# A four-layer graph network on one core: the edge loop spread over more steps, second maps set apart, aggregates with a second buffer

## The reference, cut to what matters

```python
h = act(edge_scalars @ fcW1 * c)
w = h @ fcW2 * c                      # 192 weights for each edge
xs, xv = f_s[edge_src], f_v[edge_src] # first map of the source node
edge_feat = products of w, xs, xv and edge_attr   # 4 x 96 numbers
agg = jax.ops.segment_sum(edge_feat, edge_dst, num_segments=n)
conv = second map of agg
x = _layernorm(x + combine(self map of x, conv), axis=-1)
```

## Time and profile before

| | |
|---|---|
| median of 3 runs | 4588.22 us (4581.89 to 4590.08) |
| the profiled execution | 4606.82 us, span 4605.1 us |
| busy shares of the span | PE 77%, PEld 69%, DVE 59%, ACT 47%, POOL 52% |
| instructions | 99292 |
| TensorE's mean granted clock | 0.902 |
| edge stages, about | 70 to 800, 1210 to 1965, 2315 to 3080, 3410 to 4200 us |

### The profile page before, as it was taken

How to read it: one execution, slowest core, us unless ns; L and a number is a source line. 1 busy time by engine, 2 the same in 40 slices (tenths; PEclk the granted TensorE clock), 3 DMA queues, 4 the chain that set the end, 5 groups by cost and what they waited for, 6 DMA issues and landing times.

```text
span 4605.1 us, 99292 instructions
## 1 busy us (share of the span) xinstructions
PE 3557.9 (77%) x23534; PEld 3169.8 (69%) x23534; DVE 2735.3 (59%) x11380; ACT 2167.5 (47%) x5622; POOL 2414.6 (52%) x2869
## 2 busy tenths in 40 slices
PE   3677778566577777889967777789987887787887
PEld 2677767566576777777756666677766777777776
DVE  3455555788644444578844444458865555555887
ACT  0223223566422222367733333347764444445888
POOL 1555555788555555466645555530015555555776
PEclk9788888888888888899978888989989999999999
DMA  9411122777411111278821111238861111113776
GB/s 355 157 42 43 45 47 60 233 252 255 129 32 39 42 42 42 53 249 291 289 57 37 40 43 42 47 117 298 298 193 31 34 40 41 40 43 128 259 261 231
DMA packets 424040, 572.49 MB, mean 124 GB/s; under 512 B 219010, under 2 KB 242340, under 8 KB 419618
## 3 DMA queue, kind: packets, MB, share of 16 engines
q1 hardware_dynamic: 295170, 322.46, 23.2%
q0 software_dynamic: 81680, 114.98, 9.8%
q10 hardware_dynamic: 47088, 133.90, 7.4%
HBM read 356.10 MB, written 233.79 MB: 128 GB/s over the span
## 4 chain that ended last, share of the span: by engine, by line
PE 37%; another core or an unknown queue 18%; ACT 13%; issue 13%; DVE 12%; DMA 4%; ACTq 2%; DVEq 1%; POOL 0%; SPq 0%; POOLq 0%
PE bank L799 7%; ACT arena L1071 5%; PE bank L830 4%; PE bank L828 4%; PE bank L838 3%; PE bank L806 3%; DVE stats L1425 3%; PE bank L852 3%; PE bank L829 2%; PE bank L787 2%; ACT nT L1045 2%; DVE arena L1418 1%; PE bank L907 1%; DVE mv L1436 1%
## 5 line engine op out<-in xcount | busy, mean ns | idle before, releaser
L584 POOL DMA_INDIRECT aggregates<-arena,meta x784 | 798.9, 1019 | 1083.4 <-ACT arena L993 344.1
L1071 ACT ACTIVATE arena<-arena,shift,rstd 128x160 f32<-128x160 f32 x1600 | 697.2, 508 | 64.9 <-DVE shift L1356 63.0
L571 POOL DMA_INDIRECT xg<-x_after,meta x588 | 584.3, 994 | 264.7 <-issue 258.4
L799 PE MATMUL bank<-same_all,msg 128*128 (+1 forms) x4704 | 644.6, 291 | 1.2 <-issue 1.2
L799 PEld LDWEIGHTS bank<-same_all,msg 128*128 128x128 f32 x4704 | 615.6, 209 | 1.7 <-issue 0.4
L1272 DVE SCALAR_TENSOR_TENSOR carry<-carry,meta,bank 128x3 f32<-128x3 f32 x784 | 170.7, 218 | 669.1 <-ACT arena L978 402.6
L978 ACT ACTIVATE arena<-bank 128x381 f32<-128x381 f32 x784 | 368.5, 492 | 357.9 <-remote 199.2
L828 PE MATMUL bank<-w,arena 128*128 128x98 f32 (+1 forms) x1568 | 373.7, 324 | 179.7 <-issue 89.2
L806 PE MATMUL bank<-nT,weights 128*128 128x128 f32 x1176 | 230.4, 308 | 345.2 <-ACT nT L972 269.5
L828 PEld LDWEIGHTS bank<-w,arena 128*128 128x128 f32 x1568 | 297.0, 218 | 283.7 <-issue 231.7
L1425 DVE BATCH_NORM_STATS2 stats<-arena 128x6 f32<-128x160 f32 x1600 | 453.5, 314 | 41.9 <-DVE arena L1418 10.0
(11 more groups left out here) (169 smaller groups left out, 7842.9 us busy)
## 6 DMA issues: line engine op xcount, KB each, us to landing
arena<-aggregates SPq DMA_DIRECT2D x400, 324.0 KB
x_after<-arena ACTq DMA_DIRECT2D x300, 320.0 KB
arena<-x_after SPq DMA_DIRECT2D x300, 320.0 KB
aggregates<-arena ACTq DMA_DIRECT2D x25, 1296.0 KB
arena<-nodes SPq DMA_DIRECT2D x100, 320.0 KB
out<-arena SPq DMA_DIRECT2D x100, 320.0 KB
same_all<-sorted_dst SPq DMA_DIRECT2D x7, 1792.0 KB, 13.3
aggregates<-arena,meta POOLq DMA_INDIRECT x784
```

The source lines that it names most:

```text
L571: gp.indirect_dma_start(xg[:, k % XGR, 4 + t * F:4 + (t + 1) * F], None, xtab[l], at).then_inc(gathered[k], 16)
L584: gp.indirect_dma_start(agg, at, tot[:, kk % TRING, t, 0:AW], None, bounds_check=NP - 1, oob_is_err=False).then_inc(spread[kk], 16)
L799: last = nc.tensor.matmul(bank[5 + t][:, c * P:(c + 1) * P], sent[:, c * P:(c + 1) * P], same_all[:, bass.ds(here[t], P)], start=True, sto ...
L1071: last = nc.scalar.activation(row, row, ACT.Identity, bias=shift[:, kk, t:t + 1], scale=rstd[:, kk, t:t + 1])
```

## The change

TensorE's step now works on four pairs: T and H of pair q, W and F of pair q-1, S of pair q-3, M0 and M1 of pair q-4, in the order T, S, M0, W, F, M1, H. ScalarE's step follows it: T's copy of pair q, the sums of pair q-3, the totals of pair q-4 (the first ahead of layer 3's gating of pair q-1, the second behind it), and the activation of pair q last. `aggT` has two buffers, and the copy into it waits for M of pair q-5 in place of q-3. VectorE completes the messages of pair q first and mends pair q-2 (before: pair q-1) behind that. The loops of TensorE and ScalarE are two steps longer, VectorE's one. GpSimd's and SyncE's code is the same. No product, copy or transfer is added or removed.

```diff
-                    has_new, has_old = within(q, 0, NPAIR), within(q, 2, NPAIR + 2)
+                    given, made = within(q, 0, NPAIR), within(q, 1, NPAIR + 1)
+                    sent, mapped = within(q, 3, NPAIR + 3), within(q, 4, NPAIR + 4)
...
-                        pe.wait_ge(msg_ready, edge_count(l, q - 2))
+                        pe.wait_ge(msg_ready, edge_count(l, q - 3))
...
-                            wait(pe, summed_out[t], edge_count(l, q - 3))
-                            wait(pe, mended[t], edge_count(l, q - 3))
+                            wait(pe, summed_out[t], edge_count(l, q - 4))
+                            wait(pe, mended[t], edge_count(l, q - 4))
...
+                    def second_map(t):
+                        pe.wait_ge(summed_out[t], edge_count(l, q - 4))
+                        pe.wait_ge(mended[t], edge_count(l, q - 4))
...
+                        mm(part_of(0, first), aggT[:, k2, t, 0, :], rows_of(0, first), start=True, stop=False)
...
+                    if mapped:
+                        second_map(0)
+                    if made:
+                        k1 = (k - 1) % 2
+                        pe.wait_ge(h_act, edge_count(l, q - 1))
+                        wait(pe, wy_ready, edge_count(l, q - 2))
...
+                        last.then_inc(w_ready, 1)
+                        pe.wait_ge(turned_out, edge_count(l, q - 1))
...
+                        last.then_inc(f_ready, 1)
+                    if mapped:
+                        second_map(1)
+                    if given:
                         pe.wait_ge(turned_out, edge_count(l, q))
                         wait(pe, h_act, edge_count(l, q - 1))
...
-                steps(pe, 0, NPAIR + 2, EDGE_STEADY, edge_products)
+                steps(pe, 0, NPAIR + 4, EDGE_STEADY, edge_products)
...
-                            act.wait_ge(summed[t], edge_count(l, q - 2))
-                            wait(act, tot_ready[t], edge_count(l, q - 3))
+                            act.wait_ge(summed[t], edge_count(l, q - 3))
+                            wait(act, tot_ready[t], edge_count(l, q - 5))
...
-                        act.wait_ge(tot_ready[t], edge_count(l, q - 2))
+                        act.wait_ge(tot_ready[t], edge_count(l, q - 4))
...
-                steps(act, 0, NPAIR + 2, EDGE_STEADY, edge_copies)
+                steps(act, 0, NPAIR + 4, EDGE_STEADY, edge_copies)
...
-                        dve.wait_ge(summed_out[t], edge_count(l, q - 1))
-                        wait(dve, tot_ready[t], edge_count(l, q - 2))
+                        dve.wait_ge(summed_out[t], edge_count(l, q - 2))
+                        wait(dve, tot_ready[t], edge_count(l, q - 4))
...
-                    if within(q, 1, NPAIR):
-                        mend(0)
-                        mend(1)
                     dve.wait_ge(dprod_ready, edge_count(l, q))
                     nc.vector.tensor_reduce(msg[:, k2, :, 0, S:MF], dprod[:, :, :, :].rearrange("p t d v -> p t v d"),
                                             AX.X, ALU.add).then_inc(msg_ready, 1)
-
-                steps(dve, 0, NPAIR + (3 if l == 3 else 1), EDGE_STEADY if l else FIRST_STEADY, edge_vectors)
+                    if within(q, 2, NPAIR):
+                        mend(0)
+                        mend(1)
+
+                steps(dve, 0, NPAIR + (4 if l == 3 else 2), EDGE_STEADY if l else FIRST_STEADY, edge_vectors)
```

More of the change, by code:

```diff
@@ L788, in edge_products @@
                         last.then_inc(turned, 1)
-                    if has_old:
-                        pe.wait_ge(msg_ready, edge_count(l, q - 2))
+                    if sent:
+                        here = [((q - 3) * 2 + t) * P for t in range(2)]
+                        if not isinstance(q, int):
+                            here = [pe.snap(at) for at in here]
+                        pe.wait_ge(msg_ready, edge_count(l, q - 3))
                         if l == 0:
-                            pe.wait_ge(same_ready, (q - 1) * 2)
+                            pe.wait_ge(same_ready, (q - 2) * 2)
@@ new lines, in edge_products @@
+                    if mapped:
[4 more added lines that the diff above has]
+                        wait(pe, wy_ready, edge_count(l, q - 2))
+                        if PACKED[l]:
+                            last = nc.tensor.matmul(bank[2][:, 0:384], hT[:, k1, 0:P], fc2[l], start=True, stop=True)
+                        else:
+                            for t in range(2):
+                                last = nc.tensor.matmul(bank[2][:, t * 192:(t + 1) * 192], hT[:, k1, t * P:(t + 1) * P],
+                                                        fc2[l], start=True, stop=True)
+                        last.then_inc(w_ready, 1)
+                        pe.wait_ge(turned_out, edge_count(l, q - 1))
+                        if G == 1:
+                            wait(pe, f_free, edge_count(l, q - 2))
+                            for c in range(3):
+                                a, e = c * CH, min((c + 1) * CH, W1C)
+                                last = nc.tensor.matmul(bank[3][:, a:e], xT[:, k1, c * P:(c + 1) * P], w1[l][:, a:e],
+                                                        start=True, stop=True)
+                        else:
+                            wait(pe, f_summed, q - 1)
+                            both = lambda ap, a, e: ap.rearrange("p (g c) -> p g c", g=2)[:, :, a:e]
+                            for c, t, a, e in ((0, 0, 0, 128), (1, 0, 128, 160), (1, 1, 0, 96), (2, 1, 96, 160)):
+                                last = nc.tensor.matmul(both(bank[3 + t][:, 0:2 * F], a, e), xT[:, k1, c * P:(c + 1) * P],
+                                                        both(w1[l], t * F + a, t * F + e), start=True, stop=True)
+                        last.then_inc(f_ready, 1)
@@ L808, in edge_products @@
                         last.then_inc(h_ready, 1)
[L810 to L857, removed]
```

92 lines of the change are left out of this document (51 added, 41 removed).

## The result

The changed kernel takes **4808.66 us** (median of 4 runs, 4803.28 to 4816.22) against 4588.28: ratio 1.0484, 95% interval 1.0465 to 1.0503. It is 220 us slower; 4758 was forecast. The profiled execution took 4811.87 us, its span 4810.2, 205 more than before.

A forecast was written before the change was run, and what follows sets the result against it. It took TensorE's signals, seen late mostly when GpSimd issues transfers, to bound the kernel. Period changes of 1.65 us times 98 gave 162, the ends 8: +170 on 4588, so 4758 us, range 4440 to 4920.

The forecast's parts named there:

- The new loop: W, VectorE's products and first mend, S, M0, then W again: 6.1 us bare, against 4.4 us before.
- Lateness and clock: TensorE's signals seen late: 1.0 us in layers 0 to 2, 0.5 in layer 3; slower clock: 0.7, 0.65, 0.6, 0.5.
- The gain from cover of the inner waits: TensorE's waits for T's copy and H's activation gain 2 us or more of cover, hiding a signal 3 us late.
- rival C: No difference: GpSimd's four issues of 1.3 us and 1.9 us of signals give 7.1 us a pair; 4596 us, chance 0.10.
- Second buffer and M0 apart from M1 at 0: Second aggregate buffer and separate M0 and M1: worth nothing unless they close the loop, which they do not.
- GpSimd and SyncE at 0: GpSimd's scatters and gathers and SyncE's table loads: cost 0, with 12 us of cover.
- Layer 3: Loop through F and ScalarE's gated copies: 7.7 us bare, 8.7 a pair with late signals and clock, +0.77.
- I leave the shares as they are: TensorE's time at 1.2 GHz kept at 28, 26, 24 and 12%; its idle time gathered before S speaks for more.
- Layers 0 to 2: New periods of 7.8, 7.75 and 7.7 us a pair: +0.66, +0.22 and 0 against before.
- the ends: Filling and draining of the longer pipe: about 2 us a stage, 8 us in all.
- B: Faster: TensorE's late signals mostly gone, periods about 6.4, 6.4, 6.4 and 8.0 us; 4293 us, chance 0.28.
- D: Much slower in layer 3: F's signal late by 3 us in every step, +245 us; 5003 us, chance 0.10.

The follow-up runs named there:

- third set: Runs on one chip beside the kernel before, which took 3776.5 us there; the changed kernel, unedited, took 4445.88 us, ratio 1.1777.
- second set: Runs on one chip beside the kernel before, which took 4574.1 us there; the changed kernel, unedited, took 4807.65 us, ratio 1.0503.
- one-scatter runs: Only the first of each pair's two scatters issued: in the changed kernel 4431.84 and 4430.98 us, in the kernel before 3669.69 and 3668.90 us.
- low sets: The first and third set together, in which the kernel before took 3774.0 and 3776.5 us.
- first set: Runs on one chip beside the kernel before, which took 3774.0 us there; the changed kernel with both mends ahead of VectorE's wait for W took 3742.97 us.

## Why the forecast held, point by point

**The new loop: right.** S waits for the mending 1.6 us a pair (at least 1 was named), moving the mends alone removes the loss over the four layers together, and taking 0.3 us out shortens layers at full clock by 0.2 to 0.3. Its bare length was 6.33 where the sum had 6.1. The term that was mis-sized is the passing to TensorE: 0.1, "0 to 0.3", was put in, and S starts 0.41 us after the first mend's recorded end (1404.03 to 1404.44; 0.42 in the first turn of the changed kernel's first profile). The leg to that end, 2.9, was right.

**Lateness and clock: nearly right in size, without the view behind it.** The four measured periods are 32.2 us together, and the loop at full clock (three of 6.33 and layer 3's 7.86) is 26.85, so lateness and clock hold 5.3; my terms sum to 3.5 + 2.45 = 5.95. My bare loops were 0.85 us too short, which offsets this: 31.95 in all. Between the second and the third set the changed kernel loses 362 us, 0.92 a pair, to late signals and the clock that goes with them. The old kernel loses 798 us between the same two sets, 2.0 a pair. So the changed kernel loses half as much to late signals as the old one (that the waits now partly run beside each other would explain it, but isn't shown), and costs 669 us where signals are on time: 669 + 362 - 798 = 233, the second set's difference. The forecast's difference was right; that it was this difference of two large terms was not visible in the profile of before, which has only the second condition in it.

**The gain from cover of the inner waits: not in the time.** H no longer waits for T's copy. But with the loop gone the change is worth 24 us in the second set, and late signals and their clock again cost it 807 us (4550 less 3743). So covering T's copy and H's activation did not lower what lateness costs. GpSimd's four issues are a bound of 5.2 us a pair with signals on time; rival C's figure, those and a late signal of 1.9, is 7.1, and 7.02 and 7.05 were measured (7.22, 6.92 and 7.12 over the whole stages of layers 0 to 2; layer 3's 8.45 is another matter). This fits rival C's mechanism, as the next bound and not as that of the change; it is argued, since no run took an issue away under late signals.

**Second buffer and M0 apart from M1 at 0, GpSimd and SyncE at 0:** the 24 to 31 us that remain with the mends moved are for the whole of the change; its parts were not tried singly. With the mends moved, the second map's wait for the totals copy in layer 3 (above) shows that "worth nothing" held for the loop of the mends and not beyond it. GpSimd at 0 is borne out by the one-scatter runs in the low sets.

**Layer 3: right by luck.** I had 7.7 + 0.5 lateness + 0.5 clock = 8.7, and 8.77 was measured, from other parts. This is the timeline of the changed kernel there:

```profile
3700.89 0.36 DVE L1307 TENSOR_TENSOR arena<-bank,meta 128x192 f32<-128x192 f32 x1 [2.69 <-PE bank L836]
...
3702.80 0.68 DVE L1317 SCALAR_TENSOR_TENSOR arena<-bank,meta,arena 128x160 f32<-128x160 f32 x2 [0.89 <-ACT arena L1008]
...
3705.68 2.18 PE L800 MATMUL bank<-same_all,msg 128*128 x12 [2.08 <-DVE arena L1276]
...
3710.39 0.36 DVE L1307 TENSOR_TENSOR arena<-bank,meta 128x192 f32<-128x192 f32 x1 [4.34 <-issue]
...
3715.19 1.60 PE L800 MATMUL bank<-same_all,msg 128*128 x12 [2.09 <-DVE arena L1276]
...
3718.25 0.36 DVE L1307 TENSOR_TENSOR arena<-bank,meta 128x192 f32<-128x192 f32 x1 [2.69 <-PE bank L836]
```

A turn is 7.86 us at the full clock and 9.50 when S, M0 and W run slowly, and no signal is late in either. The third set's mean over the whole stage is 8.67, so the clock's term is 0.8, not 0.5; what the other runs have above that, 0.1, is left for lateness, not 0.5. The step that failed there is "I leave the shares as they are": the share at 1.2 GHz about doubled, from 12 to 22%, as the sentence behind it feared.

**Layers 0 to 2:** 8.09, 7.63 and 7.69 against 7.8, 7.75 and 7.7, within 0.3 each. In layer 0 the differences agree (+0.66 forecast, +0.65 measured) since both levels were 0.3 too low: the window of rows 3 gave 7.14 for a stage whose mean was 7.44.

**What the forecast lacks, 50 us:** the four periods make 182 us and not 162; the ends make 23 and not 8 (a longer pipe costs more to fill and drain than "about 2 us a stage", if all of it is that); and the profiled execution lay 19 us above the median before but 3 after, 15 us more.

**Rivals.** B did not come: the loop's lateness stayed. And where signals are on time, the changed kernel's 4446 us is under 4588, but the old one's 3776 is far lower: B took lateness off the new kernel and left the old one as it was. C and D did not come.

## What to carry to other kernels

When a loop is spread over more steps, go round each ring of waits that crosses engines and count the steps between its signal and its use: here a release (the mend) stood behind a wait for data (W) in one in-order queue, and TensorE came to need the first before it would send the second. A release that needs nothing of the new data belongs ahead of the wait for that data; those few lines were worth 257 us in the second set, and about 700 between the third set's changed kernel and the first set's version with them moved. A ring without slack can cost more than its own length: in layer 3 TensorE's clock fell in many of the turns.

## What the runs showed that was not expected

**The same kernel at 3775 and at 4580 us.** In the low sets the old kernel takes nearly 18% less time, at a granted clock of about 0.97 against 0.90. The changed kernel's loop rows say where it lies: W until L1307 takes 0.97 in the turn of the low set, and 0.98 or 1.75 in those of the other; over the 98 pairs of layer 1 the median is 0.98 in the third set and 1.53 in the first profile. The second and third sets carry the same chip number in their records, so this can't be put down to the chip. Nor do GpSimd's issues alone make signals late, as the prediction had it "mostly": in the first set's timeline above GpSimd issues without a pause, and W until L1310 takes 0.91 us there (1306.71 to 1307.62). What makes the signals late stays open. The Trainium skill (TensorE: Matmul & The Clock Gate, "The cost: per-tile semaphore tail") puts an increment at about 26 ns behind the product, with a figure fitted to products that lie side by side in the array. In the low sets TensorE's signal leaves room for that: W's recorded end is 1406.50 + 0.87 = 1407.37, and L1307 starts at 1407.47, 0.10 us later. In the second set and the first profile signals come 0.8 us and more late, which the figure doesn't cover.

**A ratio holds for its condition only**: the changed kernel is 4.8% slower in one and 17.8% in the other, while the version with the mends moved is faster in both.

**A small step in idle time, a large one in clock.** TensorE's idle time before S of 2.08 to 2.10 us goes with a clock of 0.88 to 0.89 in layer 3, and slow turns beside fast ones; at about 1.8 it was 0.99, and 0.3 us of VectorE's work became 1.1 us of period.
